# A gated MLP with nine experts on one core: the first chunk by eight plain products, and the fifth chunk's casts in another unit

## What is computed

```python
g = jnp.einsum('bsd,edf->ebsf', h, Wg)
u = jnp.einsum('bsd,edf->ebsf', h, Wu)
expert_outs = jnp.einsum('ebsf,efd->ebsd', jax.nn.silu(g) * u, Wd)
expert_output = jnp.einsum('be,ebsd->bsd', gating_probs, expert_outs)
shared = jnp.einsum('bsf,fd->bsd', jax.nn.silu(h @ Sg) * (h @ Su), Sd)
return (1.0 - sg) * expert_output + sg * shared        # added to x
```

## Time and profile before

| | us |
|---|---|
| median of 3 runs | 2105.12 |
| lowest and highest | 2104.49, 2106.05 |
| profiled execution | 2104.28 |
| its span, from the first to the last instruction | 2102.5 |
| outside the span | 1.8 |
| PE busy in the span | 2091.9 |

### The profile page before, as it was taken

One profiled execution on the slowest core, in us unless ns is written; L12 is line 12 of the kernel. 1 busy time (PEld: TensorE's weight loads), 2 busy tenths in 40 slices (PEclk: granted clock), 3 DMA queues, 4 the chain that ended last, 5 costly groups with the idle time before them and its releaser, 6 DMA issues.

```text
span 2102.5 us, 33872 instructions
## 1 busy us (share of the span) xinstructions
PE 2091.9 (99%) x9183; PEld 1718.2 (82%) x9183; DVE 1445.0 (69%) x2631; ACT 1303.4 (62%) x2334; POOL 1608.7 (77%) x1440
## 2 busy tenths in 40 slices
PE   8999999999999999999999999999999999999999
PEld 6888888888888888888888888888888888888887
DVE  7666666666766666666676666666667666666666
ACT  7777777777566555555556655555555555555554
POOL 7988887877488777777778877777777778777776
PEclk9999999999999999999999999999999999999999
DMA  6966676766545455445445446445445445545443
GB/s 229 350 236 245 227 248 224 251 222 239 204 188 210 180 207 209 180 186 209 179 189 210 179 188 229 179 187 209 179 188 210 181 187 209 201 186 209 182 185 143
DMA packets 122895, 433.98 MB, mean 206 GB/s; under 512 B 13776, under 2 KB 42064, under 8 KB 122832
## 3 DMA queue, kind: packets, MB, share of 16 engines
q1 hardware_dynamic: 122832, 433.32, 54.8%
HBM read 329.85 MB, written 103.28 MB: 206 GB/s over the span
## 4 chain that ended last, share of the span: by engine, by line
PE 99%; POOL 0%; DMA 0%; SPq 0%; DVE 0%; issue 0%; ACT 0%; DVEq 0%; ACTq 0%
PE chain_ps L697 15%; PE chain_ps L699 15%; PE chain_ps L698 15%; PE down_ps L699 8%; PE down_ps L697 8%; PE down_ps L698 8%; PE p_ps L697 6%; PE p_ps L699 6%; PE p_ps L698 6%; PE side_ps L697 4%; PE side_ps L699 4%; PE side_ps L698 4%; DMA w_raw<-w 0%; POOL w_raw L467 0%; POOL w_lo L462 0%; SPq L285 0%
## 5 line engine op out<-in xcount | busy, mean ns | idle before, releaser
L462 POOL TENSOR_TENSOR h_forms<-h_t,h_forms 128x512 fp32r<-128x512 f32 x428 | 558.9, 1324 | 267.1 <-ACT h_forms L1102 267.1
L697 PE MATMUL chain_ps<-x_hi,gate_forms 128*128 128x512 f32 x1080 | 422.7, 391 | 0.2
L699 PE MATMUL chain_ps<-x_hi,gate_forms 128*128 128x512 f32 x1080 | 420.9, 390 | 0.0
L698 PE MATMUL chain_ps<-x_lo,gate_forms 128*128 128x512 f32 x1080 | 420.7, 390 | 0.0
L462 POOL TENSOR_TENSOR h_t<-h_b,h_t 128x512 f32<-128x512 f32 x214 | 312.5, 1460 | 73.1 <-DVE h_b L1242 57.8
L1248 DVE TENSOR_TENSOR p_ps<-tap_p,chain_ps 128x512 f32<-128x512 f32 x216 | 150.3, 696 | 248.3 <-PE chain_ps L699 248.3
L1116 ACT COPY chain_ps<-chain_ps 128x512 f32<-128x512 f32 x216 | 123.1, 570 | 282.2 <-DVE h_a L1242 194.2
L1102 ACT CAST h_forms<-h_t 128x512 fp32r<-128x512 f32 x428 | 266.6, 623 | 15.4 <-POOL h_t L462 4.2
L462 POOL TENSOR_TENSOR w_lo<-w_raw,w_hi 128x1152 fp32r<-128x1152 f32 (+2 forms) x74 | 191.7, 2592 | 76.9 <-ACT w_hi L997 76.4
L697 PEld LDWEIGHTS chain_ps<-x_hi,gate_forms 128*128 128x128 f32 x1080 | 202.6, 188 | 55.1 <-ACT chain_ps L1116 5.5
L699 PEld LDWEIGHTS chain_ps<-x_hi,gate_forms 128*128 128x128 f32 x1080 | 202.7, 188 | 43.5
(11 more groups left out here) (117 smaller groups left out, 4872.9 us busy)
## 6 DMA issues: line engine op xcount, KB each, us to landing
gate_forms<-kept_gate SPq DMA_DIRECT2D x216, 896.0 KB, 7.4
down_forms<-kept_down SPq DMA_DIRECT2D x108, 896.0 KB, 4.5
kept_gate<-w_hi SPq DMA_DIRECT2D x72, 448.0 KB, 2.5
kept_gate<-w_lo SPq DMA_DIRECT2D x72, 448.0 KB, 3.1
w_raw<-w SPq DMA_DIRECT2D x72, 256.0 KB, 3.0
w_raw<-w SPq DMA_DIRECT2D x72, 128.0 KB, 2.8
kept_down<-d_hi SPq DMA_DIRECT2D x36, 256.0 KB, 2.3
kept_down<-d_lo SPq DMA_DIRECT2D x36, 256.0 KB, 2.8
```

The source lines that it names most:

```text
L462: return nc.gpsimd.tensor_tensor(dst, a, b, ALU.subtract)
L697: nc.tensor.matmul(bank, w_high, hi, start=start, stop=False, **on)
L698: nc.tensor.matmul(bank, w_high, lo, start=False, stop=False, **on)
L699: return nc.tensor.matmul(bank, w_low, hi, start=False, stop=stop, **on)
```

## The change

Chunk 0 is done by eight plain products on A11, A12, A21 and A22, and B12 is now used (it lies in a token slot of the second group). The gate sums and up sums of chunk 0 come whole out of four banks, so that nothing is tapped or added for it. Its Strassen sums are still made, since later groups read them, but by POOL, and their low parts come late on DVE. The casts of chunk 4 on ACT move from behind unit 2 into unit 3. The down weights of chunk 0 are stored ahead of its gate forms, and chunk 4's blocks are loaded later. Semaphores that counted chunk 0 (`p1_tapped`, `gate1_done`, `up1_done` and others) count one less (`PLAIN`).

```diff
-HI_IN_UNIT = {7: 9}
-HI_BEHIND_UNIT = {1: 3, 2: 4, 3: 5, 4: 6, 5: 7, 6: 8}
+HI_IN_UNIT = {3: 4, 7: 9}
+HI_BEHIND_UNIT = {1: 3, 3: 5, 4: 6, 5: 7, 6: 8}
...
             def first_keeps():
-                sp.wait_ge(w0_lo_done, 4)
-                load_blocks(0, 4)
                 sp.wait_ge(w_lo_done, 1)
+                sp.wait_ge(w1_gate_lo_done, 1)
                 load_blocks(0, 5)
-                keep_gate(0, 0)
+                sp.wait_ge(w0_lo_done, 3)
                 keep_down(0, 0)
                 sp.wait_ge(w_lo_done, 2)
                 load_blocks(0, 6)
-                sp.wait_ge(w1_lo_done, 2)
+                sp.wait_ge(w0_lo_done, 4)
+                load_blocks(0, 4)
+                keep_gate(0, 0)
+                sp.wait_ge(w1_lo_done, 1)
...
             def first_chunks():
+                plain_chunk_sums()
                 next_sums(0, 0)
-                pool.wait_ge(w1_hi_done, 1)
-                part_lo(1, A11, A12).then_inc(w1_lo_done, 1)
-                pool.wait_ge(w_hi_done, 1)
+                coefficients()
+                pool.wait_ge(w_hi_done, 2)
                 part_lo(1, S3, S4).then_inc(w_lo_done, 1)
-                coefficients()
                 next_sums(0, 1)
...
+            def plain_chunk():
+                gate0, up0, gate1, up1 = chain_ps[:, 1, :], chain_ps[:, 0, :], p53_ps[:], side_ps[:]
...
+                product(up0, made(0, A21), b11, start=True, stop=False)
+                pe.wait_ge(b12_lo_done, 1)
+                product(gate1, made(0, A11), b12, start=True, stop=False)
+                product(up1, made(0, A21), b12, start=True, stop=False)
+                product(gate1, made(0, A12), b22, start=False, stop=True).then_inc(p3_done, 1)
+                product(up1, made(0, A22), b22, start=False, stop=True).then_inc(p7_done, 1)
+                product(gate0, made(0, A12), b21, start=False, stop=True).then_inc(p2_done, 1)
+                product(up0, made(0, A22), b21, start=False, stop=True).then_inc(p4_done, 1)
...
             def first_units():
-                p1_of(0, 0)
-                p5_of(0, 0)
-                p2_of(0, 0)
-                p6_of(0, 0)
-                p3_of(0, 0)
-                p7_of(0, 0)
+                plain_chunk()
                 p1_of(1, 1)
                 p5_of(1, 1)
-                p4(0, 0, 0, first=True)
                 p6_of(1, 1)
```

More of the change, by code:

```diff
@@ L576, in coefficients, with plain_chunk_sums, step @@
                 ).then_inc(coef_steps, 1)
+            def plain_chunk_sums():
+                def step(dst, a, b, op):
+                    nc.gpsimd.tensor_tensor(raw_of(0, dst, dst), raw_of(0, a, a), raw_of(0, b, b), op).then_inc(w0_sums, 1)
+                pool.wait_ge(w0_lo_done, 2)
+                step(S1, A21, A22, ALU.add)
+                step(S3, A11, A21, ALU.subtract)
+                pool.wait_ge(w0_sums, 1)
+                step(S2, S1, A11, ALU.subtract)
+                pool.wait_ge(w0_sums, 3)
+                step(S4, A12, S2, ALU.subtract)
             def first_chunks():
+                plain_chunk_sums()
                 next_sums(0, 0)
-                pool.wait_ge(w1_hi_done, 1)
-                part_lo(1, A11, A12).then_inc(w1_lo_done, 1)
-                pool.wait_ge(w_hi_done, 1)
+                coefficients()
+                pool.wait_ge(w_hi_done, 2)
                 part_lo(1, S3, S4).then_inc(w_lo_done, 1)
-                coefficients()
                 next_sums(0, 1)
@@ L766, in p2_of @@
             def p2_of(n, k):
-                after(pe, h_lo_done[1], n)
-                opening = isinstance(n, int) and n == 0
-                product(side_ps[:], made(k % SLOTS, A12), x_of(0, B21, opening), start=True, stop=True).then_inc(p2_done, 1)
+                pe.wait_ge(h_lo_done[1], n)
+                product(side_ps[:], made(k % SLOTS, A12), x_of(0, B21, False), start=True, stop=True).then_inc(p2_done, 1)
             def p3_of(n, k):
-                pe.wait_ge(p5_tapped, n + 1)
-                opening = isinstance(n, int) and n == 0
+                pe.wait_ge(p5_tapped, n + 1 - PLAIN)
                 product(
-                    p53_ps[:], made(k % SLOTS, S4), x_of(0, B22, opening), start=False, stop=True, goes_on=True
+                    p53_ps[:], made(k % SLOTS, S4), x_of(0, B22, False), start=False, stop=True, goes_on=True
                 ).then_inc(p3_done, 1)
             def p7_of(n, k):
[L779 to L782, removed]
+                pe.wait_ge(u2_tapped, n + 1 - PLAIN)
+                opening = isinstance(n, int) and n == 1
                 product(
@@ L808, in unit @@
                 n = group(0, e, k)
-                p4(0, (k - 1) % CHUNKS, n - 1)
+                p4(0, (k - 1) % CHUNKS, n - 1, first=isinstance(n, int) and n == 2)
                 p1_of(n, k)
@@ L1262, in h1_made @@
                 dve.wait_ge(silu_done[1], n + 1)
-                dve.wait_ge(up1_done, n + 1)
+                if isinstance(n, int) and n == 0:
+                    dve.wait_ge(p7_done, 1)
+                else:
+                    dve.wait_ge(up1_done, n + 1 - PLAIN)
                 weighed(side_ps[:], silu[:, 1], side_ps[:], 0, e, 1, h1_done)
@@ L1416, in two_groups, with w_lo_of @@
                     tap(7, gp, pc - 1, is_first(ep, jp))
+            def w_lo_of(first, last, parts):
+                dve.wait_ge(w0_hi_done, parts)
+                minus(lo_of(0, first, last), raw_of(0, first, last), hi_of(0, first, last).bitcast(F32)).then_inc(
+                    w0_lo_done, 1
+                )
             def first_forms():
@@ L1424, in x_lo_of @@
                 def x_lo_of(form):
-                    dve.wait_ge(x_hi_done, FIRST_X_HI.index(form) + 1)
+                    dve.wait_ge(x_hi_done, FIRST_X.index(form) + 1)
                     minus(x_lo[:, 0, form], full[form], x_hi[:, 0, form].bitcast(F32)).then_inc(x_lo_done, 1)
[L1428 to L1435, removed]
                 def x_sum_of(i, a, b):
@@ L1441, in first_forms @@
                 w_lo_of(A11, A12, 1)
[L1442 to L1447, removed]
+                w_lo_of(A21, A22, 2)
+                dve.wait_ge(b12_hi_done, 1)
+                minus(x_lo[:, 1, B11], x[0][1], x_hi[:, 1, B11].bitcast(F32)).then_inc(b12_lo_done, 1)
                 dve.wait_ge(x_loaded[0][0], 16)
```

158 lines of the change are left out of this document (86 added, 72 removed).

## The result

| | before | changed |
|---|---|---|
| median of 16 runs, us | 2104.64 | 2108.66 |
| lowest and highest | 2104.03, 2106.05 | 2106.74, 2110.19 |
| profiled execution | 2104.28 | 2108.58 |
| its span | 2102.5 | 2106.8 |

The ratio of the changed kernel to the one before is 1.0019, with a 95% interval of 1.0012 to 1.0026: 4.0 us slower, just within the 0.2%. The interval lies wholly above 1, and the fastest run of the changed kernel is above the slowest of before, so this small loss can be told from nothing. The prediction had called it one that can't. I had forecast 2107.3 and a range of 2104.5 to 2110.2. The time lies in the range, 1.4 us above the forecast. The kernel before was run 59 times more beside the experiments; one of these runs took 3011.73 us with a granted clock of 0.655, is in no ratio and moves their median by 0.02 us.

A forecast was written before the change was run, and what follows sets the result against it. PE was taken as the bound, without a hole, from about 22 us on. A 3.6 us hole less 1.0 us gained in the opening gave +2.6 us, taken as 2107.3 us, range 2104.5 to 2110.2.

The forecast's parts named there:

- rival 2: PE's clock also falls in the hole: 2109.0 us with one slow stretch, 2110.7 with two; chance 0.15.
- The case that I had held for the likeliest: Hole in PE, opening about 1 us sooner, clock kept: 2106 to 2108.6 us; chance 0.65.
- The ring: Loop ACT, POOL, ACT, PE around chunk 4's casts, putting p6 of chunk 4 at 43.04 us instead of 39.49.
- The plain products: Opening: 24 matmuls instead of 21, 0.7 us more PE work paid from waiting; opening 1.0 us sooner.
- the first mark: Start of PE's p1 of chunk 2, at 21.78 us before; forecast at 20.75, 1.0 us sooner.
- POOL and DVE came out level: Opening: POOL's work allows p1 of chunk 2 from 20.7 us at the earliest, DVE's at 20.4 to 20.7.
- The single terms: POOL's opening steps: four sums 2.27 us, 640-column low parts 1.78, eight sums 3.87, chunk 2's low parts 2.83.
- The casts in unit 3: Moving chunk 4's casts tears a new PE hole of 3.55 us before p6 of chunk 4; taken as 3.6.
- The transfers: Later load of chunk 4's blocks and early store of the down parts: counted as 0.
- The clock: PE's clock kept at 2.4 GHz behind the hole; its fall was only a rival, chance 0.15.
- one stretch at the lower clock: A PE stretch at 1.2 GHz like the opening's 3.64 us, 8.5 matmuls, costs 1.7 us.
- The base: Time before, to which +2.6 us is added: profiled execution 2104.28 or median of three 2105.12.

The follow-up runs named there:

- run 59: No label but a count: the kernel before, unchanged, was run 59 times more beside the experiments; medians 2104.10 us (31 runs) and 2104.49 us (28 runs).
- e1: Changed kernel with chunk 4's casts put back behind unit 2; 2103.03 us, 1.1 below the kernel before.
- e3: Changed kernel with POOL's pair sums and chunk 5's sums ahead of chunk 4's low parts, casts still in unit 3; 2102.69 us, 1.4 below before.
- e8: The e3 kernel run again in the later batch; 2103.38 us, 1.1 below the kernel before.
- e2: Kernel before with only chunk 4's casts moved into unit 3; 2109.15 us, 5.0 above before.
- e4: Changed kernel with only the four pair sums ahead of chunk 4's low parts on POOL; 2104.71 us, 0.6 above before.
- e5: Changed kernel with two of the four pair sums ahead of chunk 4's low parts on POOL; 2107.51 us, 3.0 above before.
- e7: Changed kernel with four more unused sums on POOL behind chunk 4's low parts; 2111.20 us, 6.7 above before.
- e6: e3 with chunk 0's down weights stored behind its gate forms, as in the kernel before; 2103.50 us beside 2103.38 for e8.
- the second batch: Runs e5 to e8, beside which the kernel before had a median of 2104.49 us (28 runs).

## Why the prediction was right, and where it was off

The time is in the range because the range took in the lower part of rival 2. The case that I had held for the likeliest, with the clock kept, ended at 2108.6, and 2108.66 is just outside it. The ring was foreseen by its mechanism; the clock was not, and that the number was still right is partly luck.

**The plain products.** I had the first mark at 20.75 us; it came at 20.80. Such a hit is luck to some tenths: in the eight profiled executions that have this opening the mark lies between 20.27 and 21.12 us. The three more matmuls were paid out of waiting, as said. POOL and DVE came out level: `up1_made` let PE go on at 19.90 (I had 19.6 to 19.9), and p1 then came 0.33 us behind the matmul ahead of it instead of 0.23; I take the 0.1 us for a wait for POOL's low parts. The single terms were less good than their sum. POOL got chunk 1's blocks at 9.02, not at 8.63, and its four sums took 2.88 us, not 2.27; the low parts of 640 columns took 1.5 us to the next step, not 1.78, and the eight sums 3.67, not 3.87:

```profile
9.02 2.88 POOL L473 TENSOR_TENSOR w_raw<-w_raw 128x128 f32<-128x128 f32 x4 [0.84 <-DMA w_raw<-w]
...
12.73 1.57 POOL L468 TENSOR_TENSOR w_lo<-w_raw,w_hi 128x640 fp32r<-128x640 f32 x1
14.25 3.72 POOL L473 TENSOR_TENSOR w_raw<-w_raw 128x128 f32<-128x128 f32 x8
```

The errors cancelled. The times of e1, e3 and e8 agree with a gain of about 1 us (1.1 to 1.4), though each interval reaches past no change.

**The casts in unit 3.** The ring was right in its place, its order and its size: a hole of 3.55 us forecast, 3.45 measured, and from the tap at 32.02 to p6 at 42.18 the ring took 10.16 us where the terms give 10.15; the idle times were near too (POOL 3.57 us where I had about 4, ACT 4.67 where I had 4.5). e2 shows that the move alone does it, e3 that the other end of the ring undoes it, and e4, e5 and e7 that it moves with the POOL work inside it.

**The transfers.** Counted at 0, and 0 they are: e2 has the same wait without the later load, and e6 shows no cost or gain of the store.

**The clock.** This is the step that failed. The forecast had the clock kept, with a chance of 0.65, and put its fall as a rival at 0.15. I left it second since no row of before shows a fall. The rival came in: 2109.0 forecast for it, 2108.66 measured, and one stretch at the lower clock priced at 1.7 us where the trace has 1.53, some 1.3 of it for the clock itself. The price rested on 8.5 matmuls in the 3.64 us of the opening, by the pitch; the trace has eight there, since two of their steps are longer than 0.43. The rule of the Trainium skill that I had named (TensorE: Matmul & The Clock Gate, Why this matters for your kernels) pointed the right way, and the trace of the changed kernel agrees with it: matmuls at 0.42 us behind a wait of 3.3. That no row shows a fall was no evidence against it, since there is also no row of before with such a hole: the rows spoke neither for a fall nor against one. The 16 runs bear the fall out. The five with a mean granted clock of 0.998 took 2109.26 to 2110.19 us, the nine with 0.999 took 2108.17 to 2109.17, and the two with 1.000 took 2106.74 and 2108.02. The fastest is 2.1 us above the median of before; my forecast without the clock was +2.6. The other, 3.4 us above, may have had a short fall that three digits don't show.

**The base.** I had put the forecast between the profiled execution and the median of three. The median of 16 was 2104.64, nearer to the profiled one, and cost the forecast little.

## What to carry to other kernels

When an instruction moves down an in-order list, follow the work that waits for it until it comes back to the engine where it began: here ACT's cast held up POOL, whose sums held up ACT's next casts, whose tap held up PE. Such a ring sets its own time, and no slack of an engine on the way pays for it; four terms from the rows of the old trace gave its size to 0.1 us. Where an engine stands idle inside the ring, look first at whether it has work further down its own list that could be done in that time, since turning that list round (e3) cost PE nothing and closed the hole. And where a change tears a hole of some microseconds in a busy PE, price the hole and the clock behind it.

## What the runs showed of the hardware

Whether PE's clock falls depends on the hole and on the execution. With PE waiting 1.5 us (e4) the profiled execution kept 2.4 GHz, and all eleven runs had a mean granted clock of 1.000. With 2.5 us (e5) the profiled one kept it too, while seven of eleven runs had 0.999 and were 1.4 us slower than the other four. With 3.3 us (the changed kernel and e2) the profiled ones fell and ran 6 to 7 matmuls at 1.2 GHz; 14 of 16 and all nine runs had less than 1.000. With 5.0 us (e7) the profiled one ran 12 of them, and all six runs had 0.998. I had not expected a middle range in which the same program keeps the clock in one execution and loses it in the next; what decides between the two is not shown.

The spread between runs is no sign of a fall by itself. The changed kernel had 3.5 us between its 16 runs and the kernel before 2.0, but the kernel before also had 3.9 us between the 28 runs of the second batch, all with a mean granted clock of 1.000.

Behind a wait the first matmul also costs more at full clock: 0.33 to 0.34 us to the next one instead of 0.23 (e4 and e5).
